# Gathering X0 for four chunks at once: one field per gather, sixteen transposes per set of 128 samples

## The reference, cut to what matters

```
e = stack([tbl_f[ids[:, f]] for f in range(39)], axis=1)          # X0: 512 x 39 x 16
def _cin_layer(X0, Xi, W, b):                                      # W: 128 x (39 * Fi)
    return einsum('hjk,bjd,bkd->bhd', W.reshape(H, 39, Fi), X0, Xi) + b[None, :, None]
X1 = _cin_layer(X0, X0, W0, b0); X2 = _cin_layer(X0, X1, W1, b1); X3 = _cin_layer(X0, X2, W2, b2)
z  = concatenate([X1.sum(2), X2.sum(2), X3.sum(2)], axis=1)        # 512 x 384
out = relu(relu([z, dense] @ W_top1 + b) @ W_top2 + b) @ W_top3
```

## Time and profile before

| what | value |
|---|---|
| median of three runs | 704.57 us (703.93 to 705.88) |
| the profiled execution | 704.89 us, span 703.1 us, mean granted TensorE clock 0.993 |
| TensorE matmul, busy | 666.1 us, 95% of the span |
| VectorE, ScalarE, GpSimd, busy | 558.8, 501.4, 363.1 us (79%, 71%, 52%) |

### The profile page before, as it was taken

The page is one execution under the profiler, slowest core; times in us unless marked ns, Lnnn a source line. Parts: engine busy times, 40 slices in busy tenths (PEclk is TensorE's granted clock), DMA queues, the critical chain, the costliest instruction groups (busy, mean ns, idle before and its releaser), DMA issues.

```text
span 703.1 us, 15109 instructions
## 1 busy us (share of the span) xinstructions
PE 666.1 (95%) x2978; PEld 473.1 (67%) x2978; DVE 558.8 (79%) x1211; ACT 501.4 (71%) x1629; POOL 363.1 (52%) x351
## 2 busy tenths in 40 slices
PE   0399999999999999999999999999999999999998
PEld 0256777777777777777777777777777777774443
DVE  0457889999999999989999999999998999994000
ACT  0356788787888878887888787878788787983002
POOL 6868774747475656656565747474753333000000
PEclk9999999999999999999999999999999999998999
DMA  6436223222222223030313131322222220002000
GB/s 212 121 93 225 87 52 85 49 85 50 76 59 71 63 56 78 21 105 11 100 35 88 47 84 49 85 50 85 50 71 60 58 55 4 1 17 60 0 1 0
DMA packets 28094, 45.73 MB, mean 65 GB/s; under 512 B 5968, under 2 KB 9424, under 8 KB 27817
## 3 DMA queue, kind: packets, MB, share of 16 engines
q1 hardware_dynamic: 20249, 39.06, 18.5%
q10 hardware_dynamic: 2704, 5.11, 2.9%
q0 software_dynamic: 5120, 1.32, 2.0%
HBM read 40.36 MB, written 5.11 MB: 65 GB/s over the span
## 4 chain that ended last, share of the span: by engine, by line
PE 87%; DVE 4%; POOL 3%; issue 3%; DMA 1%; ACT 1%; DVEq 0%; SPq 0%; ACTq 0%; POOLq 0%
PE acc L337 14%; PE ya L360 12%; PE ya L361 11%; PE ya L362 11%; PE yd L362 8%; PE yd L360 8%; PE yd L361 8%; PE yd L432 5%; PE misc L344 4%; PE misc L322 3%; POOL emb L267 2%; DVE chain L474 2%; DVE x2t L489 1%; PE misc L329 1%; POOL prod L207 1%
## 5 line engine op out<-in xcount | busy, mean ns | idle before, releaser
L589 ACT ACTIVATE prods<-ya,x0t 128x128 f32<-128x128 f32 x1472 | 447.3, 500 | 104.5 <-PE ya L362 102.1
L474 DVE SCALAR_TENSOR_TENSOR chain<-yd,x0t,chain 128x128 f32<-128x128 f32 x768 | 219.2, 343 | 15.3 <-PE yd L362 12.5
L360 PE MATMUL ya<-w1h,x1h 128*128 128x512 f32 (+1 forms) x384 | 206.7, 538 | 0.0
L207 POOL TENSOR_TENSOR prod<-tiles,x0a 120x512 f32<-120x512 f32 x105 | 137.0, 1305 | 101.0 <-PE acc L337 94.4
L267 POOL DMA_INDIRECT emb<-in_tables,rows x160 | 159.6, 998 | 38.7 <-issue 25.7
L361 PE MATMUL ya<-w1l,x1h 128*128 128x512 f32 (+1 forms) x384 | 147.8, 385 | 0.0
L362 PE MATMUL ya<-w1h,x1l 128*128 128x512 f32 (+1 forms) x384 | 147.2, 383 | 0.0
L489 DVE TENSOR_REDUCE x2t<-prods 128x128 f32<-128x1792 f32 x64 | 129.2, 2019 | 1.5 <-DVE chain L474 0.3
L337 PE MATMUL acc<-prod,w 120*128 120x512 f32 x224 | 116.6, 605 | 11.4 <-DVE prod L207 9.4
L489 DVE TENSOR_REDUCE prods<-prods 128x128 f32<-128x1536 f32 x64 | 111.7, 1745 | 0.0
L288 POOL TENSOR_TENSOR diag<-x0t,const 128x320 f32<-128x320 f32 x64 | 46.4, 725 | 121.3 <-PE misc L344 121.3
(11 more groups left out here) (59 smaller groups left out, 435.9 us busy)
## 6 DMA issues: line engine op xcount, KB each, us to landing
tiles<-x_rows SPq DMA_DIRECT2D x112, 240.0 KB, 3.4
w<-in_w SPq DMA_DIRECT2D x2, 2496.0 KB, 12.3
x_rows<-x ACTq DMA_DIRECT2D x16, 312.0 KB
x0a<-x_rows SPq DMA_DIRECT2D x48, 80.0 KB
emb<-in_tables,rows POOLq DMA_INDIRECT x160, 2.4
prods<-in_W_top SPq DMA_DIRECT2D x2, 512.0 KB, 4.5
gram<-in_w0ab SPq DMA_DIRECT2D x1, 840.0 KB, 6.6
x<-in_W_top SPq DMA_DIRECT2D x1, 256.0 KB, 2.6
```

The lines of the kernel that those rows point to most:

```text
L207: engine.tensor_tensor(prod0[:, i % L0_PRODS, :], tiles[:, slot, :], x0a[:, :], ALU.mult).then_inc(prod0_ready, 1)
L360: pe.matmul(out, x1h[:, xs], w1h[:, cols], start=True, stop=False)
L474: dve.scalar_tensor_tensor(out, product, x, run if step else b1[:, :], ALU.mult, ALU.add).then_inc(yd_used, 1)
L589: mm = act.activation(prods[:, :, slot_of(q) + i], ya[(NA * g + k) % YA][:, i * H:(i + 1) * H], ACT.Copy, scale=turned(c)[:, g * F1 + j:g ...
```

## The change

Chunks 0 to 3 (`OLD` = 4) are gathered, widened and laid out as before. Chunks 4 to 15 form three sets m of four chunks (128 samples). A set is gathered by 39 indirect DMAs, each of 128 samples of one field, into `embs` [128 samples, 39 x 16]: 117 gathers, so 157 in all. It isn't widened. Its lay-out is 16 transposes [128 x 39] to [39 x 128], one per dimension, in four steps of four transposes (`turn_set`), each copied out by ScalarE (`evacuate_set`) into a buffer `x0` of four chunks. The table `X0_AT` says after which block each step stands (values 2 and 3 are the old lay-outs of chunks 2 and 3, then come the steps). The writes of the rows to DRAM (`write_rows`) are a step of their own in ScalarE's program (`ROWS_AT`), the turns stand at `TURN_AT`, and `SET_AT` says how many gathers of which set follow product i in chunk c of GpSimd's program. Layer 0's late places are used in chunks 0 and 3 (`LATE_L0`). `misc_free` holds TensorE before each use of `misc`; ScalarE copies out two blocks after the step, as before. TensorE's and ScalarE's programs are written out for all 16 chunks. The host arranges the row numbers for it.

```
+X0_AT = {(0, 1, 1): 2, (1, 0, 1): 3, (2, 2, 8): 4, (2, 3, 1): 5, (2, 3, 8): 6, (3, 0, 1): 7}
+TURN_AT = {(0, 2, 1): 2, (1, 1, 1): 3, (3, 1, 1): 4, (3, 3, 1): 5}
+ROWS_AT = {(3, 0, 4): 4, (3, 2, 6): 5}
+for c_ in range(SET, CHUNKS - 2):
+    TURN_AT[c_, 3, 1] = c_ + 2
+    ROWS_AT[c_, 2, 6] = c_ + 2
+for m_ in range(2, SETS + 1):
+    for s_, (g_, q_) in enumerate(((0, 1), (0, 8), (1, 1), (1, 8))):
+        X0_AT[SET * m_ - 2, g_, q_] = OLD + STEPS_X0 * (m_ - 1) + s_
+EVACUATED = 2
+SET_AT = {(0, 5): (1, 4), (0, 6): (1, 4)}
+for i_ in range(T0):
+    SET_AT[1, i_] = 1, 3 - i_ % 2
+    SET_AT[2, i_] = 1, 3
+    if i_:
+        SET_AT[3, i_] = 2, 2
+    SET_AT[4, i_] = SET_AT[5, i_] = 2, 2
+    if i_ > 3:
+        SET_AT[6, i_] = 3, 2
+    SET_AT[7, i_] = SET_AT[8, i_] = SET_AT[9, i_] = 3, 2
...
+            def gather_set(m, f_range):
+                if m > 1:
+                    pool.wait_ge(lay_done, OLD + STEPS_X0 * (m - 1))
+                for f in f_range:
+                    i = OLD * FO + (m - 1) * F + f
+                    pool.indirect_dma_start(
+                        embs[:, f * D:(f + 1) * D], None, a["tables"],
+                        bass.IndirectOffsetOnAxis(ap=rows[:, i:i + 1].bitcast(U32), axis=0),
+                    ).then_inc(set_in, 16)
...
             for c in range(CHUNKS):
-                if c + 2 < CHUNKS:
+                if c + 2 < OLD:
                     widen(c + 2)
                 for i in range(T0):
                     if c + 1 < CHUNKS:
                         multiply0(pool, c + 1, i)
                     if i in DIAG_AFTER:
                         block_diagonal(c, DIAG_AFTER[i])
-                    if c + 3 < CHUNKS and 2 * i < FO:
-                        gather(c + 3, range(2 * i, 2 * i + 2))
+                    if c == 0 and 2 * i < FO:
+                        gather(3, range(2 * i, 2 * i + 2))
+                    elif (c, i) in SET_AT:
+                        m, n = SET_AT[c, i]
+                        gather_set(m, islice(left[m], n))
...
+            def turn_set(m, s):
+                pe.wait_ge(set_in, 16 * F * m)
+                by_dim = embs[:, :].rearrange("p (f d) -> p d f", d=D)
+                for i in range(DS):
+                    mm = pe.transpose(misc[0:F, i * P:(i + 1) * P], by_dim[:, DS * s + i, :], const[:, C_ID:C_ID + P])
+                mm.then_inc(lay_done, 1)
...
+            def misc_free(at):
+                pe.wait_ge(x0_ready, done_by(X0_AT, 2, at))
+                pe.wait_ge(x0t_ready, done_by(TURN_AT, 2, at))
+                wait_done(pe, g_ready, GROUPS * at[0] + at[1] - (1 if at[2] <= G_AFTER else 0))
...
+                l0_after = L0_AFTER_0 if c in LATE_L0 else L0_AFTER
...
                         layer1_block(GROUPS * c + g, g, q)
-                        if nxt and (g, q) in l0_after:
+                        if c + 1 < CHUNKS and (g, q) in l0_after:
                             layer0(c + 1, l0_after.index((g, q)))
...
+                        if at in X0_AT:
+                            misc_free(at)
+                            if X0_AT[at] < OLD:
+                                lay_out(X0_AT[at])
+                            else:
+                                turn_set((X0_AT[at] - OLD) // STEPS_X0 + 1, (X0_AT[at] - OLD) % STEPS_X0)
+                        if at in TURN_AT:
+                            misc_free(at)
+                            turn_x0(TURN_AT[at])
+                        if q == G_AFTER and (g or c):
+                            misc_free(at)
                             gram_group(GROUPS * c + g - 1, (g - 1) % GROUPS)
...
+            def write_rows(c):
+                act.wait_ge(x0_ready, c + 1 if c < OLD else OLD + STEPS_X0 * (c // SET))
+                wait_done(act, scratch_in, 16 * c)
+                act.dma_start(chunk_rows(c).rearrange("(u j) n -> j u n", u=COPIES),
...
+            def evacuate_set(m, s):
+                act.wait_ge(lay_done, OLD + STEPS_X0 * (m - 1) + s + 1)
+                act.wait_ge(x0t_done, SET * m)
+                act.wait_ge(scratch_in, 16 * SET * m)
+                act.activation(x0[0:F, :, :].rearrange("p c (g d b) -> p d (c g) b", g=GROUPS, d=D)[:, DS * s:DS * (s + 1)],
+                               misc[0:F, :].rearrange("p (d n b) -> p d n b", d=DS, b=GB),
+                               ACT.Copy).then_inc(x0_ready, 1)
```

More of the change, by code:

```diff
@@ L14 @@
 from contextlib import ExitStack
+from itertools import islice
 import numpy as np
@@ L44 @@
 XT = 4
+OLD = 4
+SET = P // CB
+SETS = CHUNKS // SET - 1
+STEPS_X0 = 4
+DS = D // STEPS_X0
+assert OLD == SET
 W1_PARTS = 3
@@ L71, with done_by, behind @@
 L0_AFTER_0 = ((1, 3), (1, 6), (1, 9), (2, 2), (2, 5), (2, 8), (3, 1))
-LAY_AFTER, X0T_AFTER, G_AFTER = (0, 1), (1, 1), 6
-DIAG_AFTER = {0: 0, 2: 1, 4: 2, 6: 3}
-def lay_group(prev):
-    return 0 if prev else 1
+G_AFTER = 6
+LATE_L0 = (0, SET - 1)
+X0_AT = {(0, 1, 1): 2, (1, 0, 1): 3, (2, 2, 8): 4, (2, 3, 1): 5, (2, 3, 8): 6, (3, 0, 1): 7}
[18 more added lines that the diff above has]
+    SET_AT[7, i_] = SET_AT[8, i_] = SET_AT[9, i_] = 3, 2
+DIAG_AFTER = {0: 0, 2: 1, 4: 2, 6: 3}
+def done_by(table, first, at):
+    return first + sum(key < at for key in table)
+def behind(table, at):
+    c, g, q = at
+    q -= EVACUATED
+    if q < 0:
+        c, g, q = (c, g - 1, q + BLOCKS) if g else (c - 1, GROUPS - 1, q + BLOCKS)
+    return table.get((c, g, q))
 def fields_of(q):
@@ L362, in layer1_block, with chunk @@
                 pe.matmul(out, x1l[:, xs], w1h[:, cols], start=False, stop=True).then_inc(ready, 1)
[L364 to L368, removed]
+            def chunk(c):
+                l0_after = L0_AFTER_0 if c in LATE_L0 else L0_AFTER
                 for g in range(GROUPS):
@@ L403, in _ @@
             pe.wait_ge(w1_split, W1_PARTS)
[L404 to L408, removed]
+            for c in range(CHUNKS):
+                chunk(c)
             def hidden1_early(m):
@@ L591, in multiply, with chunk @@
                 mm.then_inc(ya_used, 1)
-            def chunk(c, prev, nxt, lay):
+            def chunk(c):
                 split_back(c)
@@ L596, in chunk @@
                     for q in range(BLOCKS):
+                        at = c, g, q
                         if OWNERS[q] == "A":
                             multiply(c, g, q)
[L599 to L603, removed]
+                        step, turn = behind(X0_AT, at), behind(TURN_AT, at)
+                        if step is not None and step < OLD:
+                            evacuate_layout(step)
+                        elif step is not None:
+                            evacuate_set((step - OLD) // STEPS_X0 + 1, (step - OLD) % STEPS_X0)
+                        if turn is not None:
+                            evacuate_x0t(turn)
+                        if at in ROWS_AT:
+                            write_rows(ROWS_AT[at])
+                        if q == G_AFTER + 1 and (g or c):
                             evacuate_gram(GROUPS * c + g - 1)
-                        if nxt and (g, q) == (L0_AFTER[-1][0], L0_AFTER[-1][1] - 1):
+                        if c + 1 < CHUNKS and (g, q) == (L0_AFTER[-1][0], L0_AFTER[-1][1] - 1):
                             evacuate_x1(c + 1)
@@ L677 @@
     field = np.minimum(np.arange(FP), F - 1).reshape(FO, FI)
+    ids, first = host("ids"), starts[:F].astype(np.int32)
+    old = ids[:OLD * CB].reshape(OLD, CB, F)[:, :, field].transpose(3, 1, 0, 2).reshape(P, OLD * FO)
+    sets = ids[OLD * CB:].reshape(SETS, P, F).transpose(1, 0, 2).reshape(P, SETS * F)
+    first_old = np.tile(np.repeat(first[field.T], CB, axis=0), (1, OLD))
+    first_sets = np.tile(first, (P, SETS))
     arrays = {
         "tables": np.concatenate(tables),
-        "ids": host("ids").reshape(CHUNKS, CB, F)[:, :, field].transpose(3, 1, 0, 2).reshape(P, CHUNKS, FO),
-        "first_row": np.repeat(starts[field.T].astype(np.int32), CB, axis=0),
+        "ids": np.concatenate([old, sets], axis=1),
+        "first_row": np.concatenate([first_old, first_sets], axis=1),
         "const": constants(),
```

47 lines of the change are left out of this document (19 added, 28 removed).

## The result

| | before | after |
|---|---|---|
| median of four runs each on one chip | 705.23 us (703.93 to 706.75) | 726.48 us (722.28 to 727.95) |
| the profiled execution | 704.89 us, span 703.1 | 725.55 us, span 723.7 |
| mean granted TensorE clock in it | 0.993 | 0.993 |

What follows compares the result with a forecast made beforehand. TensorE, busy 95% of the span, was taken to bound the kernel. 3.4 + 3.0 + 9.1 + 6.9 - 6.3 = 16.1 us slower, 721.0 profiled, 720.7 median; likeliest case 713 to 728, 8 in 10 706 to 730.

Steps and rivals of the forecast that it cites:

- The signs named for it: Chunks without steps at 36.5, TensorE waits on copies some 9 us, layer 0 waits on GpSimd 11 to 12, chunk 3 at 46.
- Chunk 3: Chunk 4's rows come late, then GpSimd sets the pace: waits of 4.7 and 3.4 us, chunk 46.4, 9.1 slower.
- the steps of chunks 6 and 10: Four steps each, waits for copies of 0.6, 1.4, 0.6 us: 40.8 a chunk, 3.5 slower each, 6.9 together.
- chunk 0: Four gathers between GpSimd's products 5 and 6 delay product 6 to 80.4, so TensorE waits 3.4 us.
- chunk 1: Forecast of the difference for this chunk: 0.
- the plain chunks: Eight chunks without any step: lay-out gone, VectorE's waits return, 36.52 us each, 0.79 gained in each, 6.3 in all.
- dear transposes: Rival: a step of four transposes costs 1.1 us instead of 0.6, six us more, 726.7; chance 0.08.
- the clock: Rival: TensorE's clock falls in the long waits of chunks 0 and 3, up to 8 us more, 723 to 729; chance 0.11.
- Steps: Four transposes taken at 0.6 us (0.55 to 1.1), twelve steps 7.2; waits for copies 0.6 or 1.4 each.
- Chunk 2: Steps at (2, 8), (3, 1), (3, 8) with waits of 0.6, 0.9, 1.1 us: 40.35, 3.0 slower.
- VectorE's waits: Chunk 14 loses 0.75 us to them; forecast to return in plain chunks. Rival, they don't: 709 to 714, chance 0.07.
- The start: The stretch up to chunk 0: no difference forecast.

Runs made afterwards that it cites:

- e5: Changed kernel without the eight gathers of set 1 in chunk 0, three a product in chunk 1 instead; 722.25 us in one execution.
- e1: Kernel before with the chunk loops of TensorE and ScalarE written out; median 704.38 us, ratio 1.0012.
- e3: Kernel before with TensorE's chunk loop alone written out; 702.77 us in one execution.
- e6: Changed kernel with no gathers in chunk 3 (set 2 in chunks 4 and 5) and its layer 0 tiles later; 723.79 us.
- e12: The change from the ninth chunk on instead of the fifth, two sets, set 1's gathers over chunks 1 to 5; median 703.85 us, ratio 1.0005 against before.
- e4: Changed kernel with ScalarE's equal chunks (4 and 5, 7 to 9, 11 to 13) in hardware loops; 720.54 us.
- e7: Changed kernel with the steps of sets 2 and 3 mostly one block later and ScalarE's copies one block behind instead of two; 721.86 us.
- e8: Changed kernel with the changes of e5, e6 and e7 together, set 1's steps moved likewise; median 712.24 us, ratio 1.0096 against before.
- e2: Kernel before with ScalarE's chunk loop alone written out; 705.24 us in one execution.
- e9: Kernel before with 48 waits on an already standing semaphore in ScalarE's program ahead of its first lay-out copy; 705.05 us in one execution.
- e11: e8 with set 1's and set 2's gathers spread anew and ScalarE's loops of e4; median 708.65 us, ratio 1.0060 against before.

## Why the prediction was right, and where it was off

Slower was right, and so was the time within its range; the causes forecast are those that the experiments could take away one by one. The signs named for it came: with 0.3 for the edge of each, the waits on copies before the steps come to 9.6 us (some 9 forecast) and those of layer 0 on GpSimd to 10.6 (11 to 12).

That the sum comes so near, 16.1 against 15.5, is luck in part. Chunk 3 was put 1.8 and the steps of chunks 6 and 10 1.5 too high, chunk 0, chunk 1 and the plain chunks 0.7, 0.7 and 1.1 too low. By the number alone two rivals, dear transposes with 726.7 and the clock with 723 to 729, lie nearer to 726.48 than the forecast does. The first is out, since a step turned out cheap; the second came true in some executions (both below).

- **Chunk 0** (+3.4 forecast, though 80.4 less 77.13 is 3.3). The wait was right (3.14, with the 0.3 at its edge 3.4), and e5 takes it away. What failed is that I stopped at the tile: the late tile makes X1 late, and chunk 1's first block waits 1.56 more. Together these gathers cost 5.1, by e5. The chunk grew by only 4.1, because without them it takes 38.87, less than the 39.81 of before; so it does in e1 to e3 (39.2 to 39.5), which start late as well.
- **Chunk 3** (+9.1). The mechanism was right, the size too high: the wait on the first product was 2.57, with its edge 2.9, instead of 4.7. I had the rows issued 7.3 us into the chunk and 8.65 from there to the product; they were issued at 178.87, 6.1 into it, and the product began at 186.87, 8.0 later. The four waits at GpSimd's pace were 0.53 to 0.66 each, 3.6 with their edges against 3.4. e6 brings 4.7 us of it back, of which chunks 4 and 5 lose 2.7.
- **Steps.** The waits were right and the steps too dear. With their edges the waits at (0, 8), (1, 1), (1, 8) are 0.6, 1.5 and 0.6, against 0.6, 1.4 and 0.6. The copy took 0.66, as taken. A step was taken at 0.6, at least 0.55. Measured as the prediction measured the turn, one that waits for nothing costs 277.42 - 276.52 - 0.46 = 0.44 (e12). Four steps are so 0.6 cheaper, most of the 0.8 by which chunks 6 and 10 stayed under 40.8. One transpose is recorded with 0.27 us; this agrees with the 275 ns that the Trainium skill gives for a 128x128 one ("TensorE: Matmul & The Clock Gate", Part 4). But each begins 0.11 after the one before it, so that four don't take the estimated 1.1 that adding these times up gives. Chunk 2 came out as forecast in its sum.
- **Plain chunks.** 36.65 instead of 36.52: VectorE's waits do come back, as chunk 14 had said: 12 waits on its products in the list above.
- **Chunk 1** (0). It has one more wait, 0.30 on VectorE's sums. That this is an echo of the late chunk 0 isn't shown: e4, whose chunk 0 is late too, takes 37.33 there, and e5, whose chunk 0 isn't, 38.06.
- **The clock.** In the profiled execution of the changed kernel the granted clock stayed at 1.00 behind the waits of chunks 0 and 3 that this rival named. At the start, which it hadn't named, it fell. Windows of the changed kernel (busy us by engine, granted clock, DMA share, GB/s):

```profile
44.00:50.00 6.00, 1.47 (x33) 1.30 (x32) 0.56 (x1) 1.80 (x3) 3.63 (x5) 1.00 0.06 6
50.00:52.00 2.00, 1.97 (x7) 1.64 (x8) 0.00 (x0) 0.50 (x2) 0.85 (x1) 0.52 0.48 122
52.00:54.00 2.00, 2.00 (x7) 1.60 (x6) 0.45 (x2) 1.28 (x4) 0.00 (x0) 0.62 0.19 46
54.00:56.00 2.00, 2.00 (x11) 1.62 (x10) 1.89 (x8) 1.62 (x6) 0.00 (x0) 1.00 0.54 132
86.00:89.00 3.00, 3.00 (x12) 2.15 (x13) 0.49 (x2) 1.84 (x5) 2.51 (x3) 1.00 0.39 108
```

After 4.56 us without work the blocks run at 1.2 GHz, 0.43 from one matmul to the next instead of 0.23, for some three microseconds: about 1.5 us (an estimate). In other executions the clock did fall behind the named waits. In e10, which is the changed kernel but for 48 waits in ScalarE's program, it fell behind both:

```profile
87.02 1.28 PE L412 MATMUL acc<-prod,w 120*128 120x512 f32 x2 [3.14 <-POOL prod L253]
88.00:91.00 3.00, 3.00 (x8) 2.34 (x7) 0.11 (x1) 2.50 (x6) 2.39 (x3) 0.50 0.73 222
...
189.04 1.12 PE L412 MATMUL acc<-prod,w 120*128 120x512 f32 x2 [2.45 <-POOL prod L253]
190.00:193.00 3.00, 3.00 (x9) 2.36 (x8) 0.12 (x1) 1.68 (x6) 2.55 (x3) 0.54 0.58 163
```

It did so too in chunk 0 of e4, e6 and e7, in chunk 3 of e5 and e7, and behind the waits for gathers in e5 and e8 (2.56 and 2.59). The granted clock behind each was 0.50 to 0.54. The Trainium skill's rule that an idle TensorE goes to half clock ("TensorE: Matmul & The Clock Gate", Part 1) is borne out here and at the start, and not by the waits of 3.14 and 2.57 in the changed kernel's own profile. So this rival was wrong for that execution and right for others.

- **The start** (0 forecast, +6.5 in the profiles). I read the start off one execution and took it as given. The late signal of the second lay-out makes up 4.0 of it, the lay-out that comes 2.5 us later (44.06 instead of 41.60) the rest; of this, the first lay-out's copy, late in the same way (24.09 instead of 22.25), makes up 1.8. The wait turns up in the kernel before too (e1, e2, e3, e9). That these runs take no longer doesn't make it free: their ends took 93.6 to 93.7, that of the profile of before 98.27 (next point), and e9 starts 4.3 later and ends in 4.6 less. Over the timed kernels, the difference of the medians follows that of chunks 0 to 14, not that of the starts: +0.2 for -0.6 in e1, +6.6 for +6.8 in e8, +3.4 for +3.6 in e11, -0.6 for -1.5 in e12. Their intervals, 1.5 to 3 us either way, leave room for a part of the start.

  For the changed kernel itself the medians differ by 21.3 where its chunks lose 15.5. Its four executions took 722.28, 725.55, 727.42 and 727.95 us at granted clocks of 0.998, 0.993, 0.984 and 0.981: the lower the clock, the longer. At one and the same clock, 0.998, its one execution took 720.5 (span) and 16 of before, from the experiments, 699.6 to 703.5, in the middle 701.6: 18.9. So some 2.4 of the remaining 5.8 us go with the clock. The last 3.4 would fit a start that is that much later, but with one execution this isn't shown, and what the start costs stays open. By the chunks alone the forecast was 0.6 too high.
- **The end.** The 98.3 and 96.8 us from chunk 15 on hold a stretch at half clock in the perceptron; in e1, e5, e9 and others there is none, and the end takes 93.6 to 93.9. The changed kernel ends in 96.8 and e10, whose code differs only in ScalarE's 48 waits at the start, in 93.9. So the stretch comes and goes between executions, and the 1.5 is most likely not the change's.

## What to carry to other kernels

A batch that is four times as large saves instructions, but it has to be complete before the first use: count what the engine that gathers must fit in between, from which point on, and what its products are needed for. Taking gathers from one chunk moved the wait to the next (e5, e6) until there were five chunks to spread them over (e12), and then the saving, 0.65 us a chunk less 1.0 for each set's chunk with steps, was too small to measure. When a tile comes late, follow it one stage further, to the start of the next chunk; before a stretch of the profile is taken as fixed, look at it in a second execution; and price a row of small matmuls by the distance of their starts, not by the time recorded for one.

## What the runs showed that I had not expected

- The signal of the second lay-out came 2.0 to 4.0 us after the modelled end of its last matmul in 13 of 14 profiled executions, and ScalarE, whose wait the profile puts down to "remote", stood still until then. Neither the length of ScalarE's program, nor 48 more instructions in it, decided it. Its cause is open.
- Behind the same wait of 3.14 us, in chunk 0, the granted clock stayed at 1.00 in the changed kernel and fell to 0.50 in e10; it fell behind waits as short as 2.45 (e10, chunk 3) and stayed behind 2.57 (the changed kernel).
- The perceptron, with nearly the same code in all kernels, has a stretch at 0.50 in some executions and none in others: the end takes 96.8 to 100.1 us with it and 93.6 to 93.9 without.
